# A one-layer decoder block: another order of the last three head groups, rope angles on GpSimd, and part of the first residual in advance

## The reference, cut to what matters

```python
x = x + latent_attention(layernorm(x))     # 128 heads of 4 content + 64 rope columns, latent 64; the rope part of q is x @ Wq_rope
x = x + cross_attention(layernorm(x), ctx) # 32 heads of 16, 8 key heads, rotary angles from integer positions
x = x + ffn(layernorm(x))                  # x @ base_w + bias + a top-2 mixture of rank-16 adapters
```

## Time and profile before

| | us |
|---|---|
| median of 3 runs | 869.03 (868.4 to 870.11) |
| the profiled execution | 867.85 |
| its span, first to last instruction | 865.9 |
| mean granted TensorE clock, share of full speed | 0.978 |

### The profile page before, as it was taken

One profiled execution on the slowest core, in us unless ns is written; L12 is line 12 of the kernel. 1 busy time (PEld: TensorE's weight loads), 2 busy tenths in 40 slices (PEclk: granted clock), 3 DMA queues, 4 the chain that ended last, 5 costly groups with the idle time before them and its releaser, 6 DMA issues.

```text
span 865.9 us, 17867 instructions
## 1 busy us (share of the span) xinstructions
PE 803.9 (93%) x5624; PEld 395.2 (46%) x5624; DVE 647.9 (75%) x1209; ACT 568.5 (66%) x1045; POOL 582.8 (67%) x492
## 2 busy tenths in 40 slices
PE   4999999999999999999999999999848688999986
PEld 3464444444454444444444444444313344555433
DVE  7866777767677888777888767788787567888754
ACT  4757777777777777777777777777530465555641
POOL 7747888888788878888888878885543223333210
PEclk9999999999999999999999999999978799999999
DMA  8344455434334332434333433432130000000001
GB/s 334 110 166 146 92 156 169 139 85 112 101 90 105 85 108 78 107 97 123 85 82 91 113 104 89 109 89 56 29 88 0 1 1 3 15 13 15 13 13 37
DMA packets 51227, 74.69 MB, mean 86 GB/s; under 512 B 9968, under 2 KB 33520, under 8 KB 50672
## 3 DMA queue, kind: packets, MB, share of 16 engines
q1 hardware_dynamic: 51184, 74.18, 30.7%
HBM read 38.16 MB, written 18.87 MB: 66 GB/s over the span
## 4 chain that ended last, share of the span: by engine, by line
PE 84%; DVE 8%; ACT 2%; issue 2%; DMA 1%; SPq 1%; POOL 0%; DVEq 0%; ACTq 0%
PE PS L1200 39%; PE PS L1152 8%; PE PS L1236 7%; PE PS L1266 6%; PE PS L1268 6%; PE PS L1283 5%; PE PS L1411 2%; PE PS L1325 1%; PE PS L1418 1%; PE PS L1380 1%; PE PS L1397 1%; PE PS L1426 1%; PE PS L1456 1%; DVE xm L1027 1%; PE PS L1244 1%
## 5 line engine op out<-in xcount | busy, mean ns | idle before, releaser
L492 POOL TENSOR_TENSOR Pl<-PR,Ph 128x512 f16<-128x512 f32 x254 | 285.8, 1157 | 24.7 <-ACT Ph L668 24.7
L661 ACT ACTIVATE PR<-PS 128x512 f32<-128x512 f32 x256 | 152.6, 597 | 135.0 <-PE PS L1268 128.5
L795 DVE TENSOR_REDUCE mneg<-PS 128x4 f32<-128x512 f32 x256 | 174.6, 684 | 38.2 <-PE PS L1236 34.7
L1200 PE MATMUL PS<-XTh,Wh 128*128 128x512 f16 x512 | 194.5, 380 | 0.0
L1200 PE MATMUL PS<-XTh,Wl 128*128 128x512 f16 x512 | 193.7, 378 | 0.0
L1200 PE MATMUL PS<-XTl,Wh 128*128 128x512 f16 x512 | 193.5, 378 | 0.0
L783 DVE SCALAR_TENSOR_TENSOR QS<-PS,QC 64x512 f16<-64x512 f32 x256 | 175.5, 686 | 18.0 <-ACT QC L593 10.9
L593 ACT ACTIVATE QC<-PS 64x512 f16<-64x512 f32 x256 | 150.7, 589 | 10.6 <-PE PS L1200 4.3
L668 ACT ACTIVATE Ph<-PR 128x512 f16<-128x512 f32 x256 | 139.3, 617 | 0.0
L474 POOL TENSOR_TENSOR Wh<-Wraw,wscale 128x1024 f16<-128x1024 f32 x32 | 60.6, 1893 | 70.8 <-PE PS L1200 67.5
L1236 PEld LDWEIGHTS PS<-KC,QC 112*128 112x128 f16 x1024 | 78.8, 97 | 62.2 <-issue 2.7
(11 more groups left out here) (213 smaller groups left out, 1163.4 us busy)
## 6 DMA issues: line engine op xcount, KB each, us to landing
Wraw<-in_wqr SPq DMA_DIRECT2D x32, 512.0 KB, 4.6
QS<-QC SPq DMA_DIRECT2D x64, 256.0 KB, 3.2
head_outputs<-OS SPq DMA_DIRECT2D x256, 40.0 KB
q_content_parts<-stg SPq DMA_DIRECT2D x12, 256.0 KB, 2.8
k_content_parts<-stg SPq DMA_DIRECT2D x12, 256.0 KB, 3.1
QC<-q_content_parts SPq DMA_DIRECT2D x128, 24.0 KB
KC<-k_content_parts SPq DMA_DIRECT2D x32, 96.0 KB
xs<-in_x SPq DMA_DIRECT2D x8, 256.0 KB, 4.5
```

Of the source, the lines that this page charges most:

```text
L492: nc.gpsimd.tensor_tensor(Pl[:, b], PR[:, b % 4], Ph[:, b], ALU.subtract).then_inc(s_pl, 1)
L661: nc.scalar.activation(PR[:, b % 4, :], PS[:, bB[b % 2], :], ACT.Exp, scale=ATT_SCALE).then_inc(s_e, 1)
L795: nc.vector.tensor_reduce(mneg[:, par, b // 4, :, b % 4], PS[:, bA[b % 2], :].rearrange("p (j k) -> p j k", j=GH), AX.X, ALU.max, negate=T ...
L1200: last = mm(PS[:, bQ[c % 2], :], wt[:, par, k, p * P:(p + 1) * P], xt[:, k, sl], start=(k == 0 and n == 0), stop=(k == KT - 1 and n == 2))
```

## The change

The last three groups (29, 30, 31) no longer run each with both halves in turn. Their six halves, now called jobs, run as group 29, 30, 31 for batches 0-3, then 31, 30, 29 for batches 4-7. Job 60 (group 31, batches 0-3) is the last of its kind, and three jobs for batches 4-7 follow. The weights of group 29 are stored to DRAM in split form and read back for the last job. The low parts of the weights of groups 30 and 31 are made by halves on POOL, the high ones on ACT. Contents are loaded per job, so five DMAs per half instead of five per step. SP gathers the last quarter in two parts: batches 0-3 after `outputs` of job 60, batches 4-7 at the end. Quarters 0 to 2 of batches 4-7 are multiplied and added to x in advance (`output_part`, `x1_part`, line numbers of which don't exist before), between the scores of the last two jobs; their last quarter follows inside the loop over units, at u = 5, 8, 11 and 15. `angles` is made by POOL in the prologue, with 24 instructions, each waited for. Three of four low weight parts of the second half move from DVE to POOL, inside the loop at u = -3, 1 and 2 (`split_low`), and three of four high ones to ACT at u = -6. The tiles of the second part lie over other tiles of the first than before. Within `project` the four products with the low weights come last. All other halves keep their order and their instructions.

The diff, cut to its core:

```diff
+NH = 2 * NG
+QG = NG // KT
+LG = 3
+G0 = NG - LG
+LATE = NH - 2 * LG
+TURN = LATE + LG
+Job = namedtuple("Job", "g t n r p s k w")
+def job(h):
+    if h < LATE:
+        g, t, k = h // 2, h % 2, h // 2 % 2
+    else:
+        g = G0 + h - LATE if h < TURN else NG - 1 - (h - TURN)
+        t, k = h // TURN, (0, 2, 1, 3)[h % 4]
+    return Job(g, t, h, h // 2, h // 2 % 2, h % 2, k, g % 2)
...
+BY_DVE = range(LATE - 3, TURN - 4)
...
+        LOWS_AT = {-3: 0, 1: 1, 2: 2}
+        LATER = {5: 4, 8: 5, 11: 6, 15: 7}
...
+            def late_contents(j):
+                sp.wait_ge(s_b, 4 * (j.n - 3))
+                sl = slice(j.t * HALF, (j.t + 1) * HALF)
+                for i in range(GH):
+                    r = CROW + CR * i
+                    sp.dma_start(QC[r:r + CR, j.p, j.s, i, :], YD[j.g * GH + i, :, sl]).then_inc(s_yl[j.n % 4], 16)
+                if j.k >= 2:
+                    sp.wait_ge(s_kc, 4)
+                sp.dma_start(kc(j.k)[CROW:MROW, sl], XD[j.g * GH:(j.g + 1) * GH, :, sl].rearrange("h r k -> (h r) k")
+                             ).then_inc(s_yl[j.n % 4], 16)
...
+            def late_half(h):
+                if h == LATE:
+                    sp.wait_ge(s_ws, G0 + 1)
+                    sp.dma_start(WD[0], W16[:, G0 % 2]).then_inc(s_wst, 16)
+                    w_in(NG - 1, G0 % 2)
+                maxima(job(h - 2))
+                if h == NH - 2:
+                    sp.wait_ge(s_q, 2 * h)
+                    sp.wait_ge(s_wst, 16)
+                    sp.dma_start(W16[:, G0 % 2], WD[0]).then_inc(s_wr, 16)
+                q_again(job(h - 1))
+                if h + 1 < NH:
+                    late_contents(job(h + 1))
+                outputs(job(h - 4))
+            def gather(T, j, x0, x1, done):
+                src = OD[T * QG:(T + 1) * QG].rearrange("g r j b q -> g r j (b q)")
+                rows = slice(j * P // GH, (j + 1) * P // GH)
+                sl = slice(x0 * S, x1 * S)
+                sums = src[:, VC * j + HD:VC * (j + 1), j, sl].to_broadcast([QG, HD, (x1 - x0) * S])
+                sp.dma_start(U[rows, T, sl], src[:, VC * j:VC * j + HD, j, sl]).then_inc(done, 16)
+                sp.dma_start(SU[rows, sl], sums).then_inc(done, 16)
...
+            def half_quarter(t, j):
+                for s in range(2):
+                    sp.wait_ge(s_od[s], 64 * (NG if t else (TURN + 1 - s) // 2))
+                sp.wait_ge(s_un, B * (KT - 2) + B // 2 * (t + 1))
+                gather(KT - 1, j, t * B // 2, (t + 1) * B // 2, s_ue if t else s_ud[KT - 1])
...
+            late_contents(job(LATE))
+            for h in range(LATE, NH):
+                late_half(h)
+            maxima(job(NH - 2))
+            outputs(job(NH - 4))
+            q_again(job(NH - 1))
+            maxima(job(NH - 1))
             for j in range(GH):
-                gather(KT - 1, j)
-            sp.wait_ge(s_q, 4 * NG)
+                half_quarter(0, j)
+            outputs(job(NH - 3))
+            outputs(job(NH - 2))
+            sp.wait_ge(s_b, 4 * NH)
             sp.dma_start(lb_sb[:], lb).then_inc(s_ffn, 16)
             sp.dma_start(bias[:], bb.to_broadcast([P, DM])).then_inc(s_ffn, 16)
+            outputs(job(NH - 1))
+            for j in range(GH):
+                half_quarter(1, j)
...
+            def late_rest(g):
+                par, n = g % 2, g - G0
+                pool.wait_ge(s_wa, n)
+                for p in range(2):
+                    w = Wraw[:, par, :, p * P:(p + 1) * P]
+                    nc.gpsimd.tensor_tensor(w, w, wscale[:].to_broadcast([P, KT, P]), ALU.mult).then_inc(s_wd2, 1)
+                    pool.wait_ge(s_wd2, 2 * n - 1 + p)
+                    nc.gpsimd.tensor_tensor(Wl[:, par, :, p * P:(p + 1) * P], w, Wh[:, par, :, p * P:(p + 1) * P], ALU.subtract
+                                            ).then_inc(s_wp, 1)
...
             pool.wait_ge(s_kvl, 1)
             nc.gpsimd.memset(V[:, 0, :, :, HD], 1.0)
             nc.gpsimd.memset(V[:, 1, :, :, HD], 0.0).then_inc(s_zero, 1)
+            def angles():
...
+                pool.wait_ge(s_pos, 16)
+                pool.wait_ge(s_zero, 4)
+                link(nc.gpsimd.tensor_copy(posf[:], posi[:]))
+                link(nc.gpsimd.tensor_tensor(ang[:], posf[:, :, None].to_broadcast([P, B, HF]),
+                                             invf[:, None, :].to_broadcast([P, B, HF]), ALU.mult))
+                for i, quarter in enumerate((0.0, 0.25)):
+                    r = red[:, i]
+                    link(nc.gpsimd.tensor_scalar(turns[:], ang[:], 1 / (2 * math.pi), quarter, ALU.mult, ALU.add))
+                    link(nc.gpsimd.tensor_scalar(turns[:], turns[:], MAGIC, None, ALU.add))
+                    link(nc.gpsimd.tensor_scalar(turns[:], turns[:], MAGIC, None, ALU.subtract))
+                    src = ang[:]
+                    for part in TWO_PI:
+                        link(nc.gpsimd.tensor_scalar(fold, turns[:], part, None, ALU.mult))
+                        link(nc.gpsimd.tensor_tensor(r, src, fold, ALU.subtract))
+                        src = r
+                    link(nc.gpsimd.tensor_scalar(r, r, quarter * 2 * math.pi, math.pi, ALU.add, ALU.min))
+                    last = nc.gpsimd.tensor_scalar(r, r, -math.pi, None, ALU.max)
+                    if i == 0:
+                        link(last)
+                last.then_inc(s_red, 1)
+            angles()
             pool.wait_ge(s_vl, B)
-            pool.wait_ge(s_zero, 4)
+            pool.wait_ge(s_red, 1)
             values(0, 0)
...
+            pool.wait_ge(s_vg, 1)
+            nc.gpsimd.memset(KC2[96:P], MS).then_inc(s_zero, 1)
+            pool.wait_ge(s_zero, 5)
+            for i in range(2):
+                nc.gpsimd.tensor_copy(KC2[0:RD, i, :], KS[0:RD, :]).then_inc(s_kc, 1)
+            pool.wait_ge(s_kc, 4)
...
+            for h in range(LATE, NH):
+                p_low(job(h - 3))
+                if h < TURN - 1:
+                    late_rest(job(h).g + 1)
+                if h == LATE:
+                    values(G0 - 1, (G0 - 1) % 2)
+                else:
+                    late_values(job(h - 1))
+                if h == TURN:
+                    nc.gpsimd.memset(xvz[:], 0.0).then_inc(s_xvz, 1)
+                if h == TURN + 1:
+                    pool.wait_ge(s_kvo, B)
+                    pool.wait_ge(s_xvz, 1)
+                    nc.gpsimd.tensor_copy(xvz[:, :, :, 0:XVC], xv[:]).then_inc(s_xvz, 1)
+                if h == TURN + 2:
+                    pool.wait_ge(s_red, 1)
+                    nc.gpsimd.tensor_copy(id16, ident[:]).then_inc(s_kx, 1)
+            late_values(job(NH - 1))
+            pool.wait_ge(s_q, 2 * NH)
+            nc.gpsimd.memset(kst[:, :, :, :, X3], MS).then_inc(s_kx, 1)
+            for n in range(NH - 3, NH):
+                p_low(job(n))
...
+            def split_low(n):
+                l, w, h = ((wol, xwo_sb, woh), (bwl, bw_raw, bwh), (agl, ag_raw, agh))[n]
+                pool.wait_ge(s_xh, n + 2)
+                nc.gpsimd.tensor_tensor(w[:], w[:], wscale[:].to_broadcast(list(w.shape)), ALU.mult).then_inc(s_xw, 1)
+                pool.wait_ge(s_xw, n + 1)
+                nc.gpsimd.tensor_tensor(l[:], w[:], h[:], ALU.subtract).then_inc(s_xl, 1)
...
+            def late_high(g):
+                par = g % 2
+                act.wait_ge(s_w[par], 16 * (g // 2 + 1))
+                act.wait_ge(s_q, 2 * (LATE + g - 1 - G0))
+                if g == NG - 1:
+                    act.wait_ge(s_wst, 16)
+                nc.scalar.activation(Wh[:, par], Wraw[:, par], ACT.Copy, scale=WS).then_inc(s_wa, 1)
...
+            q_high(job(NH - 1), 1)
+            p_high(job(NH - 3))
             act.wait_ge(s_wx, 16)
-            act.wait_ge(s_ffn, 48)
-            act.wait_ge(s_b, 8 * NG)
-            for h, w in ((Wxh, wx_raw), (woh, xwo_sb), (bwh, bw_raw), (agh, ag_raw)):
-                nc.scalar.activation(h[:], w[:], ACT.Copy, scale=WS).then_inc(s_xh, 1)
-                if h is Wxh:
-                    act.wait_ge(s_red, 1)
-                    nc.scalar.activation(sincos[:].rearrange("p a b f -> p (a b f)"), red[:].rearrange("p a b f -> p (a b f)"),
-                                         ACT.Sin).then_inc(s_sc, 1)
+            act.wait_ge(s_q, 2 * NH)
+            split_high(0)
+            for n in (NH - 2, NH - 1):
+                for b in range(4):
+                    exps(job(n), b)
+                p_high(job(n))
+            act.wait_ge(s_red, 1)
+            nc.scalar.activation(sincos[:].rearrange("p a b f -> p (a b f)"), red[:].rearrange("p a b f -> p (a b f)"),
+                                 ACT.Sin).then_inc(s_sc, 1)
...
+                if u == FIRST + 2:
+                    act.wait_ge(s_ffn, 48)
+                    act.wait_ge(s_pv, NH)
+                    for n in range(1, 4):
+                        split_high(n)
...
+            def x1_part(v):
+                dve.wait_ge(s_o0, v - B // 2 + 1)
```

(111 more changed lines are left out.)

710 lines of the change are left out of this document (355 added, 355 removed).

## The result

The changed kernel takes 885.99 us (880.16 to 888.27), the kernel before 868.71 in the same runs: ratio 1.019, 95% interval 1.0149 to 1.0231. The forecast was 854.9 us, range 847 to 863. It came out on the other side, 17 us slower, and 31 us from the forecast.

A forecast was written before the change was run, and what follows sets the result against it. PE was taken as the bound, busy 803.9 of 865.9 us, with time to win where it idled before 702 us. Terms -23.1 + 2 + 3.5 + 3 + 0.5 = -14.1 took 869.03 to 854.9 us, range 847 to 863.

The forecast's parts named there:

- The reordered halves: Last halves up to `x1(0)`: the DRAM round trip gets cover, so `x1(0)` ends 21.8 us earlier.
- The last halves, +0.5: Six last halves: SP's issues (8.57 of 8.76 us) and POOL's work just fit, +0.5 us (0 to +7).
- D: Rival, last halves: SP's 8.57 of 8.76 us doesn't hold, six halves 1.2 us late each, +7, 861.5 us; chance 0.08.
- From `x1(0)` to the anchor: Batch 0's norm, query projection and rotation, batch 1's norm: 22.8 us instead of 24.1, plus 2 for the clock.
- the anchor: Start of the second batch's projection, from which both kernels do the same work; forecast 23.1 us early.
- Locks of the second piece, +3: Unit 1: POOL's `split_low(1)` instructions hold up DVE's through their shared port, +3 us (0 to 10, third piece included).
- The products in the loop, +3.5: Loop over units: PE gets four products back, 4 x 0.87 us, without cover, +3.5 us.
- Rival B: Loop over units: the locks cost the whole 10 us instead of 3, nothing else changes, 862 us; chance 0.12.
- Angles, 0: Prologue: the 24 angle instructions on POOL, 9.1 us, are hidden in its idle time, cost 0.
- E, the slower side, 0.08: Rival, prologue: small chained POOL instructions cost as much as a full `p_low`, prologue ends 16 us later, 871 us; chance 0.08.
- C, the clock stays up: Rival: with the 10.51 us gap under 1, PE's clock does not fall before 702 us, 848 us; chance 0.12.
- The chance of 0.90 for faster: Whole kernel: probability given to its being faster by more than 0.2% (1.7 us).

The follow-up runs named there:

- split_dve: The changed kernel with the low parts of three weights moved back from POOL to DVE: 880.44 us, ratio 1.0141 to the kernel before.
- after_again: The changed kernel itself, unchanged, timed again beside its variants: 882.18 us, ratio 1.0184 to the kernel before.
- x1_early: The changed kernel with DVE's additions x1(4) to x1(7) moved from the unit's end to right behind its two row maxima: 868.87 us, ratio 1.001.
- before_angles: The kernel before with only the rotation angles moved to POOL (24 instructions in place of DVE's 20): 868.14 us, ratio 0.9991.
- three_edits: The changed kernel with x1_early, split_dve and the two 512 KB transfers put behind the small ones in SP's queue: 860.82 us, ratio 0.9904.
- one_early: The changed kernel with one addition alone, x1(6) in unit 11, moved ahead: 881.65 us, ratio 1.0149 to the kernel before.

## Why the prediction was wrong

*The reordered halves: right.* The forecast had `x1(0)` end 21.8 us earlier. Measured 15.9, and 5.4 of the missing 5.9 are the stall of half 58. The round trip is hidden as worked out: PE is busy for 28.8 of the 29.6 us from 605 to 634.6.

*The last halves, +0.5: wrong.* I priced SP's time of issue, 8.57 of 8.76 us, and that held. I did not price what the two added transfers of 512 KB do to a 4 KB transfer right behind them. +5.4 in the trace; inside my bound of +7, by another mechanism than D's.

*From `x1(0)` to the anchor: wrong by its order.* I let `k_rope(1)` run ahead of `split_low(0)`, having priced locks only for the second and third piece. Forecast 24.8 us (22.8 and 2 for the clock), measured 29.1; with the weights back on DVE 24.1 (split_dve). The row was at hand; what I did not do was lay POOL's and DVE's unit -3 side by side.

*Locks of the second piece, +3: right as far as can be told.* `pn` took 2.00 us and `U<-U,SU` 3.18. Units 0 to 4 took 21.2 us (20.3 in after_again) instead of 18.7, with the four divisions in it; the share of the locks alone was not measured.

*The products in the loop, +3.5: the step that failed.* "PE gets four products back, 4 x 0.87", and of DVE's additions nothing. The products and additions themselves cost 6.3 us (x1_early), 2.8 more than that: two of the four cost 1.0 each, and those at units 5 and 8, where DVE is fuller (busy 8.8 of 10 us from 680 to 700), 3.2 and 1.2. But a product also takes a PSUM bank, and in this kernel the next matmuls into the bank wait until its reader is through. The reader stood last in DVE's unit, behind an operation that waits for PE's next unit. That adds some 15 us by the timings (19.7 in the first trace), about half of all that is missing. Rival B named DVE's fixed order but priced only the locks, at 7 us more. The diff shows this wait in plain sight: `take(bF[1], s_x1, v + 1)` makes the next user of bank 7 wait for `x1(v)`. In the profiled execution 9.7 of the missing 33 us were lost ahead of the anchor, by the two steps above, and 23.4 behind it.

*Angles, 0: right* (before_angles). *E, the slower side, 0.08:* fell with them; the kernel was slower for causes that no rival had. *C, the clock stays up:* wrong for this kernel; from 650 to 700 it stood between 0.62 and 0.89.

The chance of 0.90 for faster rested on one large gain and many small costs, each priced alone. With the three waits cut (three_edits) the kernel takes 860.8 us, and with DVE's order mended 853.5. That this is near the forecast of 854.9 bears out the plan and not the sum: the products still cost more than their term, and two DVE edits that the forecast doesn't have pay for it. What stays open is the exact share of the clock, and the 2.4 to 4.0 us by which the half behind the large transfers is still too long in the traces of three_edits and its variants; no better place for them was tried.

## What to carry to other kernels

When work moves into a tight loop, follow the buffer it takes and not only its duration: who reads it, where that reader stands in its engine's order, and who needs the bank next. Four additions of 0.7 us at the end of a unit instead of its middle cost 15 us. A small transfer on the critical path must not be issued just behind large ones, from whatever queue, and moving the large ones moves the wait to whoever needs them; where two engines share a lock, lay their orders side by side for every unit, not for the one that looks busy.

## What was not expected of the hardware

- Two transfers of 512 KB made a 4 KB transfer land after 5.8 us instead of 1.8 (DMA share 0.98), and after 6.3 when another engine's queue had issued them (PE's wait 3.28 us against 3.59).
- After idle stretches of 3.9 us the clock fell to its lower level for the matmuls that follow: 0.43 us apart instead of 0.22, in one_early for all twelve. Between two executions of one kernel the time from unit 0 to 31 moved by 6.3 us, at other clocks (0.90 and 0.67 from 720 to 730 us).
- With 22 matmuls that nobody reads, in idle time, the clock of a stretch was 1.00 instead of 0.59, and they cost nothing: 3.0 us less from `x1(0)` to unit 0 in the trace.
